# Attention edges of a graph network: products with y in cyclic order, some kept in PSUM, narrower maps, weights split over the rows of the array

## What is computed

```python
def _cg_tp(s, v, y0, y1, w_ss, w_sv, w_vs, w_vv0, w_vv1):
    out_s = concat([w_ss * s * y0, w_vv0 * dot(v, y1) / SQRT3])
    out_v = concat([(w_sv * s) * y1, w_vs * v * y0, w_vv1 * cross(v, y1) / SQRT2])
    return (out_s, out_v)

msg_s = (s_n @ Ws_src)[src] + (s_n @ Ws_dst)[dst]
msg_v = (v_n @ Wv_src)[src] + (v_n @ Wv_dst)[dst]
w1 = rbf @ W_rbf
m1_s, m1_v = _cg_tp(msg_s, msg_v, y0, y1, *split(w1))
a = (m1_s @ W_alpha).reshape(e, H, AS_)
a = where(a > 0, a, 0.2 * a)
a = sum(a * alpha_dot, axis=-1)
val_s = m1_s @ Ws_val
val_v = (m1_v @ Wv_val) * sigmoid(val_s @ Wg)[..., None]
val_s = sigmoid(val_s)
m2_s, m2_v = _cg_tp(val_s, val_v, y0, y1, w2_ss, w2_sv, w2_vs, w2_vv0, w2_vv1)
h = concat([m2_s @ Ws_vlin, m2_v @ Wv_vlin])
agg = segment_sum(segment_softmax(a, dst) * h, dst)
out = node + concat([agg_s @ Wps, agg_v @ Wpv])
```

## Time and profile before

| | |
|---|---|
| median of 3 runs | 9351.54 us (9351.42 to 9352.2) |
| the profiled execution | 9350.73 us, its span 9349.0 us |
| busy share of the span | PE 88%, PEld 70%, DVE 86%, ACT 57%, POOL 62% |
| constants, input and tables | about 0 to 228 us |
| attention edges | about 228 to 5322 us |
| softmax | about 5322 to 5456 us |
| aggregate | about 5480 to 6345 us |
| output, second layer's tables | about 6345 to 6690 us |
| conv edges, then the end | about 6690 to 9130, to 9349 us |

### The profile page before, as it was taken

The page is one execution under the profiler, slowest core; times in us unless marked ns, Lnnn a source line. Parts: engine busy times, 40 slices in busy tenths (PEclk is TensorE's granted clock), DMA queues, the critical chain, the costliest instruction groups (busy, mean ns, idle before and its releaser), DMA issues. The chain is left out here.

```text
span 9349.0 us, 200867 instructions
## 1 busy us (share of the span) xinstructions
PE 8247.1 (88%) x48376; PEld 6585.1 (70%) x48376; DVE 8021.4 (86%) x21707; ACT 5330.8 (57%) x17719; POOL 5808.5 (62%) x5949
## 2 busy tenths in 40 slices
PE   5999999999999999999999947775688888888885
PEld 2788888888888888888888836663355555555555
DVE  3899999999999999999999865554599999999993
ACT  1566666666666666666666611111377777777771
POOL 0776666666666666666666347770277777777760
PEclk5999999999999999999999979995699999999995
DMA  1443333333333334343333336660233333333330
GB/s 64 107 106 104 103 104 103 104 103 104 102 104 102 104 102 104 102 105 102 105 102 104 85 101 177 177 179 13 52 91 89 89 89 89 89 89 89 88 80 17
DMA packets 932683, 916.70 MB, mean 98 GB/s; under 512 B 370528, under 2 KB 734688, under 8 KB 931744
## 3 DMA queue, kind: packets, MB, share of 16 engines
q1 hardware_dynamic: 690208, 498.68, 19.4%
q0 software_dynamic: 241920, 413.20, 18.1%
HBM read 762.86 MB, written 148.44 MB: 97 GB/s over the span
## 5 line engine op out<-in xcount | busy, mean ns | idle before, releaser
L464 POOL DMA_INDIRECT ae_gsrc<-tab_src,ae_idx x1616 | 1641.9, 1016 | 1281.1 <-DVE ae_msg L583 567.0
L1096 POOL DMA_INDIRECT ce_node<-tab_conv,ce_idx x1808 | 1708.4, 945 | 1059.9 <-issue 645.5
L467 POOL DMA_INDIRECT ae_gdst<-tab_dst,ae_idx x1616 | 1819.6, 1126 | 538.6 <-issue 538.6
L1186 PE MATMUL psum<-ce_prod,ce_plain 128*128 128x384 f32 x3616 | 1540.5, 508 | 337.7 <-DVE ce_prod L1159 275.7
L1171 ACT ACTIVATE ce_prod<-ce_raw,ce_y 128x64 f32<-128x64 f32 x5424 | 1464.4, 333 | 0.0
L596 PE MATMUL psum<-pack_sb,ae_rbfy 80*128 80x352 f32 x3232 | 1161.5, 461 | 21.1 <-DVE ae_minus L494 13.2
L616 PE MATMUL psum<-pack_sb,ae_first_t 128*128 128x288 f32 x3232 | 1118.4, 428 | 41.3 <-ACT ae_first_t L689 8.8
L1169 ACT ACTIVATE ce_prod<-ce_raw,ce_y 128x160 f32<-128x160 f32 x1808 | 752.8, 416 | 528.3 <-DVE ce_raw L1118 528.3
L1188 PEld LDWEIGHTS psum<-ce_prod,ce_plain 128*128 128x128 f32 x3616 | 688.0, 190 | 479.9 <-issue 2.1
L681 ACT ACTIVATE ae_mapped<-psum 128x192 f32<-128x192 f32 x808 | 267.6, 331 | 1287.0 <-PE psum L618 1287.0
L903 POOL TENSOR_TENSOR ag_exval<-ag_val,alpha 128x256 f32<-128x256 f32 (+1 forms) x904 | 638.3, 726 | 403.6 <-DMA ag_val<-h_dram 399.1
(11 more groups left out here) (169 smaller groups left out, 21056.3 us busy)
## 6 DMA issues: line engine op xcount, KB each, us to landing
ag_val<-h_dram SPq DMA_DIRECT2D x452, 320.0 KB, 3.2
h_dram<-ae_values SPq DMA_DIRECT2D x404, 320.0 KB
ae_rbf<-in_rbf SPq DMA_DIRECT2D x404, 160.0 KB
ce_query<-in_query SPq DMA_DIRECT2D x452, 128.0 KB
ae_y<-in_y SPq DMA_DIRECT2D x404, 128.0 KB
ce_node<-tab_conv,ce_idx POOLq DMA_INDIRECT x1808
ae_gsrc<-tab_src,ae_idx POOLq DMA_INDIRECT x1616
ae_gdst<-tab_dst,ae_idx POOLq DMA_INDIRECT x1616
```

What stands on the lines that cost most here:

```text
L464: pool.indirect_dma_start(gsrc[t.slot4][:, k, :], None, g["tab_src"], bass.IndirectOffsetOnAxis(ap=idx[t.pair][:, t.odd, k:k + 1], axis=0))\
L467: pool.indirect_dma_start(gdst[t.slot4][:, k, :], None, g["tab_dst"], bass.IndirectOffsetOnAxis(ap=idx[t.pair][:, t.odd, 4 + k:5 + k], axi ...
L1096: pool.indirect_dma_start(node[t.slot8][:, k, :], None, g["tab_conv"], bass.IndirectOffsetOnAxis(ap=idx[t.slot8][:, k:k + 1], axis=0))\
L1186: pe.matmul(b_a[t.slot], plain[t.slot4][:, k, :], prod[t.slot][:, k, 96:480], start=(k == 0), stop=False, skip_group_check=True)
```

## The change

The message's vector part is multiplied with y1 at three offsets of a row of y that repeats itself cyclically (1, 2, 3, 1, 2). That gives the terms of the dot product (`diag`) and both halves of the cross product (`plus`, `minus`) before the weights are applied, so `wy` has 224 columns in place of 352. `minus`, the rows of y (`ya`, `yb`, `yc`) and `adot` lie in PSUM bank 7, which DVE alone uses; `b_h` shrinks to bank 6 and is filled in two halves. The radial values lie in 32 rows (16 of them times y0, 16 plain) for two k at a time, and the four weight matmuls of a tile use alternate groups of 32 rows, all at one place in PE's program. The values' s times y1 parts move behind the maps, as y enters there by linearity; the leaky part of the logits is a relu on ACT plus a linear part that is folded into the map (`m1_0`, four more columns), and the maps are 196, 96 and 96 columns. In the second round all three blocks have 128 rows, every matmul has 96 columns, and the matmuls of a tile come a body later and stand between the transposes. `gated` lies in the space of the nodes, so the nodes are loaded again in the aggregate; the square of y1 for every edge (`yy`) is computed once in `constants` from a load of all y. The order inside the vector part of h is x, head, channel, for which POOL reads a widened copy of alpha (`wide`) that ACT makes.

The diff, cut:

```diff
@@ constants
+                sp.dma_start(yraw[:, :, :], io["yall"]).then_inc(loaded, 16)
...
+                link(dve.tensor_tensor(ysq[:, :, :], yy4[:, :, 1:4], yy4[:, :, 1:4], ALU.mult))
+                link(dve.tensor_reduce(g["yy"][:, :], ysq[:, :, :], AX, ALU.add))
@@ attention_edges, DVE
-                def products(t, half):
...
+                        for d, out in enumerate((diag[:, :, 0:3, :], plus[:, :, :, :], minus)):
+                            ins = dve.tensor_tensor(out, v, cyclic(ya, d), ALU.mult)
+                        ins.then_inc(outer_done, 1)
...
+                        dve.tensor_tensor(gated[t.slot4][:, :, 0:8:2, :], comps(mapped[t.slot][:, :, 68:196]),
+                                          gated[t.slot4][:, :, 12:13, :].to_broadcast([P, 4, 4, CV]), ALU.mult)\
+                            .then_inc(gate_done, 1)
...
+                        dve.wait_ge(pe_weights, t.n + 1)
...
+                        dve.tensor_tensor(out[:, :, CS:96], b_w[:, :, P:160], dot[:, :, :], ALU.mult).then_inc(first_done, 1)
@@ attention_edges, PE
-                        pe.matmul(b_m[:, i, 0:288], first_t[1][:, e], w("m1_1"), start=True, stop=False)
-                        pe.matmul(b_m[:, i, 0:192], first_t[0][:, e], w("m1_0"), start=False, stop=False)
-                        ins = pe.matmul(b_m[:, i, 192:288], first_t[2][0:V3, e], w("m1_2"), start=False, stop=True)
+                        pe.matmul(b_m[:, i, 0:196], first_t[0][:, e], w("m1_0"), start=True, stop=False)
+                        pe.matmul(b_m[:, i, 196:292], first_t[1][:, e], w("m1_1"), start=False, stop=False)
+                        ins = pe.matmul(b_m[:, i, 164:260], first_t[2][0:V3, e], w("m1_2"), start=False, stop=True)
                     ins.then_inc(pe_mapped, 1)
+
+                def values_of(t, half):
+
+                    wait(pe, values_kept, 2 * t.n + half)
+                    for i in range(2):
+                        e = slice(P * (2 * half + i), P * (2 * half + i) + P)
+                        pe.matmul(b_h[:, i, 0:96], second_t[0][:, e], w("m2_0"), start=True, stop=False, skip_group_check=True)
+                        pe.matmul(b_h[:, i, 96:192], second_t[1][:, e], w("m2_1"), start=False, stop=False, skip_group_check=True)
+                        ins = pe.matmul(b_h[:, i, 32:P], second_t[2][:, e], w("m2_2"), start=False, stop=True, skip_group_check=True)
+                    ins.then_inc(pe_values, 1)
...
-                        pe.wait_ge(weighted, 2 * t.n + 1)
-                        weights(t, 1, 0)
+                    t = m + -4
+                    if t.inside(SUPER):
+                        pe.wait_ge(kept2, 3 * t.n + 3)
+                        values_of(t, 0)
...
+                        wait(pe, first_done, t.n)
+                        for k in (0, 2, 1, 3):
+                            q, e = 64 * t.slot + 32 * (k // 2), P * (k % 2)
+                            ins = pe.matmul(b_w[:, k, :], rbfy_both[q:q + 32, e:e + P], w("wy")[q:q + 32, :], start=True, stop=True)
+                        ins.then_inc(pe_weights, 1)
@@ attention_edges, ACT
+                    t = m + -4
+                    if t.inside(SUPER):
+                        wait(act, values_done, t.n - 1)
+                        wait(act, stored[t.slot4], 16 * t.quarter)
+                        keep_values(t, 0)
...
+                        for k in range(4):
+                            ins = act.activation(second[t.slot][:, k, 32:224].rearrange("p (b c) -> p b c", c=CV), gated[t.slot4][:, k, 0:12:2, :],
+                                                 ACT.Identity,
+                                                 scale=y[t.slot8][:, k, 0:1])
+                        ins.then_inc(scaled, 1)
+                    t = m + -3
+                    if t.inside(SUPER):
+                        keep2(t, 2)
@@ attention_aggregate
+                sp.dma_start(g["nodes"][:, :, :], io["x"]).then_inc(nodes_in, 16)
...
+                    pool.wait_ge(ex_done, t.n + 1)
+                    pool.tensor_tensor(exval[t.slot4][:, :, CS:C].rearrange("p k (x c) -> p k x c", c=AV),
+                                       val[t.slot8][:, :, CS:C].rearrange("p k (x c) -> p k x c", c=AV),
+                                       wide[t.slot4][:, :, :].unsqueeze(3).to_broadcast([P, 4, 3 * H, AV]), ALU.mult)\
+                        .then_inc(weighted, 1)
```

450 lines of the change are left out of this document (228 added, 222 removed), and 6 rows, old and new, of the table PACK.

## The result

The changed kernel takes 9369.29 us (median of 19 executions, 9366.18 to 9376.17), the kernel before 9351.43 (19 executions beside it). The ratio is 1.0019, 95% interval 1.0012 to 1.0026: 0.19% slower, just inside the 0.2% that the prediction called no difference. Forecast were 9024 us and a range up to 9230.

A forecast was written before the change was run, and what follows sets the result against it. PE bound the kernel before; after, a PE-ACT circle of 11.59 us plus 0.15 made 11.74 us a tile against 12.61, 351 us less over 404 tiles; with 23 added elsewhere, 9024 us, range 8790 to 9230.

The forecast's parts named there:

- The circle: Edge stage: PE and ACT wait for each other in a round of 11.59 us a tile, which sets the rate.
- the 0.15: Edge tile: estimate for three engine loops lying close together and for returns of the loop, added to 11.59 us.
- The sum: Edge tile: 9.13 us of PE work and some 2.5 of PE waiting for ACT, 11.59 together.
- Rival C: Edge stage: gaps in PE's work let the clock fall to 0.50; 20.8 us a tile, 12,680 us, chance 0.04.
- DVE: 10.6 to 11.1 forecast: Edge stage: DVE's work a tile in us, 8260 elements in 28 instructions plus up to 0.5 more.
- The room for DVE in the circle: Edge tile: DVE lets the weights' product be through by 4.9 us, and PE asks for it at 9.0.
- POOL: right: Edge stage: eight gathers a tile, 10.0 to 11.0 us in all, below what sets the rate.
- The 20 us: Constants: loading all y, its squares and sums, and small steps add 20 us on the path.
- its 9 us for the load of y: Constants: loading all y, 3.3 MB, takes 9 us, taken from 5.7 MB landing after 15.8 us.
- inside the bound: Aggregate: the second multiplication's new form costs between -0.1 and +0.5 us a step; 0 to +45 us, taken as 2.
- 0.90 for faster: Whole kernel: chance that the change makes it faster; same had 0.04, slower 0.06.
- Rival D: Edge stage: an unseen ACT or DVE wait makes the round 12.1 to 12.5 us; 9220 us, chance 0.12.

The follow-up runs named there:

- The exchanged order: Changed kernel with ACT's third copy of `turn2` put ahead of its four multiplications by y0: 9131.96 us, ratio 0.9765.
- the halved multiplications: Changed kernel with two of ACT's four multiplications by y0 left out (k = 2 and 3): 9136.24 us, ratio 0.9772.

## Why the prediction was wrong

**What bounded the kernel: right.** PE was the bound before, and its busy time fell by 672 us. The stretch after the second round is what the prediction described: the narrow maps, `turn2`, the weights in 1.03.

**The circle: the mechanism right, the sizes 0.5 us short.** The waits that it named are there: 1.20 at the second `turn` (forecast 1.5) and 0.20 to 0.28 at the second half of the second round (forecast 0.4). The one of 0.49 at the first `turn` it did not name. The exchanged order and the halved multiplications show that this circle sets the rate: with half of them the tile fell to 11.49. The legs can be read off ACT, which starts each:

```profile
3084.31 0.28 ACT L704 ACTIVATE ae_mapped<-psum 128x128 f32<-128x128 f32 x1 [1.85 <-PE psum L638]
...
3084.97 0.62 ACT L715 ACTIVATE ae_second_t<-psum 128x512 f32<-128x512 f32 x1
3085.44 1.50 ACT L763 ACTIVATE ae_second<-nodes,ae_y 128x192 f32<-128x192 f32 x4
3086.82 0.61 ACT L715 ACTIVATE ae_second_t<-psum 128x512 f32<-128x512 f32 x1
...
3089.49 0.38 ACT L721 ACTIVATE ae_values<-psum 128x256 f32<-128x256 f32 x1 [0.72 <-PE psum L648]
...
3096.40 0.28 ACT L704 ACTIVATE ae_mapped<-psum 128x128 f32<-128x128 f32 x1 [1.85 <-PE psum L638]
```

| leg | forecast | measured |
|---|---|---|
| ACT takes the maps out (3084.31 to 3084.97) | 0.73 | 0.66 |
| copy, four multiplications, copy, to PE (to 3087.49) | 2.54 | 2.52 |
| second turn, half of the second round (to 3089.49) | 1.82 | 2.00 |
| ACT copies it out (to 3090.10) | 0.65 | 0.61 |
| second half (to 3091.51) | 1.23 | 1.41 |
| maps, turn2, weights, maps (to 3096.40) | 4.62 | 4.89 |
| round | 11.59 | 12.09 |

ACT's legs are right to 0.07. PE's are 0.63 short, in four places:

- The second round, 0.26. A k of three matmuls of 96 columns was taken as 1.5 times the 0.41 of the earlier trace rows, 0.62. The four of a tile take 0.64, 0.67, 0.74 and 0.67 to the next start. A likely reason is that in the earlier trace rows the two matmuls of 96 follow one of 192, which covers part of the first one's start; the 0.74 stands right behind a wait.
- The weights, 0.18. Ahead of them `turn2` takes 0.54 where the same four transposes take 0.44 elsewhere (3093.07 to 3093.61, 3084.11 to 3084.55), and behind them the first pair of the maps takes 0.44 (3082.47 to 3082.91) where the second takes 0.36.
- From the last matmul of a block to ACT, 0.05 twice (0.20 for 0.15), and the second `turn` behind its wait, 0.05.
- The maps' own pace, 0.04 (0.78 a k for 0.77).

```profile
3082.47 0.60 PE L636 MATMUL psum<-pack_sb,ae_first_t 128*128 128x196 f32 x2
3082.91 0.36 PE L637 MATMUL psum<-pack_sb,ae_first_t 128*128 128x96 f32 x2
...
3084.11 0.60 PE L628 MATMUL psum<-pack_sb,ae_second 128*128 128x128 f32 x4
3084.55 0.60 PE L628 MATMUL psum<-pack_sb,nodes 128*128 128x128 f32 x4
...
3093.07 0.60 PE L628 MATMUL psum<-pack_sb,ae_second 128*128 128x128 f32 x4
3093.61 1.03 PE L685 MATMUL psum<-pack_sb,ae_rbfy 32*128 32x224 f32 x8
```

So going into and out of the weights costs 0.18 us, 73 us over the stage, which the prediction took as nothing because the earlier trace rows showed none.

The Trainium skill, page TensorEngine Tiling (Array Packing), section Tiling Modes, which the prediction weighed there, says that a change of tiling mode drains the TensorE. The trace agrees in kind, with 0.18 us where the prediction worked out 0.25 by that rule.

Against the 0.15 that the prediction added for returns of the loop (which cost nothing here), the circle is 0.36 us a tile over 11.74, 145 us. That alone would have left a time of about 9170, within the range.

**The clock: the step that failed.** The sum takes all of PE's work at the clock of 1.00, with some 2.5 us of waiting in each tile, 1.5 of it in one piece, and puts what the waits do to the clock at nothing. Rival C had the mechanism, gaps in PE's work, with a chance of 0.04 and a price of thousands of us, because it thought of one level for the whole stage. Its argument against itself counted matmul instructions in a us, and compared averages of stages: 6.8 here, more than in the aggregate, which holds its clock. What came was between: falls in four tiles of ten, 0.53 us a tile, 214 us. The average of a stage did not show it; the falls stand behind one pair of waits in the tile, and the larger of the two, 1.5 us, was in the prediction's own sum.

The Trainium skill has a like case, on a page that the prediction did not weigh: TensorE: Matmul & The Clock Gate, section A second HAM failure mode: psum-queue depth-cycling, tells of a bf16 kernel that cycles through PSUM banks, whose short idle times between groups of matmuls make the clock go to and fro between its two levels. The trace agrees in an fp32 kernel, with 0.49 and 1.20 us of waiting for the banks of the turns, and a clock of 0.50 behind them.

145 and 214 us are 359, and the profiled execution is 353 over the forecast (9376.17 us against 9023). The aggregate is 21 less than forecast; the other 15 us, the other way, lie mostly in the edges and the softmax and were not traced to a cause.

**DVE: 10.6 to 11.1 forecast, 11.45 or a little more measured** (where it sets the rate). The pace of products was right. The sum over four products was taken at 1.04 ns an element, 0.60 us, and takes 0.95 to the next start:

```profile
3053.07 1.05 DVE L583 TENSOR_REDUCE ae_second<-ae_diag 128x128 f32<-128x512 f32 x1
3054.02 0.55 DVE L590 TENSOR_TENSOR ae_path<-ae_values,psum 128x384 f32<-128x384 f32 x1
```

Two additions in its place brought what their rows promised, 158 us in a kernel where DVE was the bound. The room for DVE in the circle was right: no wait of PE for DVE in the changed kernel.

**POOL: right.** The gathers take 963 and 965 ns, near the lower value of the earlier trace rows (945). The Trainium skill's rule on the shared port (page SBUF — State Buffer, section Who interferes with whom) is that a DVE instruction with two SBUF inputs contends with a GpSimd instruction that reads SBUF, and one with at most one SBUF input, outside the 2-port modes, does not. The trace agrees in direction, since most products now read one input from PSUM. No run here changed that alone, so the cause is not shown.

**Constants and aggregate.** The 20 us were 19.1. Of the 5.7 MB behind its 9 us for the load of y, shows only the nodes' 3.9. The aggregate's form without a row costs 849 ns where the old one took 830, inside the bound; that the stage got 19 us shorter was not expected and has no explanation here.

**The chances.** 0.90 for faster rested on the sum and on the range of the sum. The step that failed was no term of it. Rival D's price does not follow from its own period, either: 12.1 to 12.5 us is 9170 to 9330, with a middle of 9250, not 9220.

## What to carry to other kernels

When a change turns an engine's full stretch into work with waits, price TensorE's clock with it: list the waits of one tile in order, and treat long ones that lie close together as a risk, whatever the stage's average (here falls stood behind 0.49 and 1.20 us, none behind 0.49 and 0.51, and in the kernel before none behind a single 1.23); if they can't be removed, work in the wait is the cheapest test and may be the remedy. Then ask of each engine off the path what its stops (at a loop's return, here 4 us) will cost on the day it becomes the bound. And take the pace of a short instruction from a run of short ones, not from one that follows a long one.

## What the runs showed of the hardware that I had not expected

- Useless work can pay: 1.3 us of it a tile, in a wait of 1.2, made the kernel 2.1% faster (9369 to 9172) by holding the clock at 1.00.
- A single wait of 1.23 us a tile did not lower the clock in the kernel before (no fall in 245 tiles); two, of 0.2 to 1.0 and 1.45 to 1.83, did in 20 of 35. In the changed kernel 0.49 and 1.20 did in 125 of 309, and 0.49 and 0.51, with half of ACT's multiplications, did not.
- DVE stops for 3.6 to 4.7 us when its loop returns, 4.0 on the mean, whether the loop is 8 or 32 tiles long (155.8 us in 39 times, 39.5 in 10); in the kernel before (`DVE ae_first L486 <- issue: 78.8, 40, 2.2`) 2.0 each. Why it doubled with the change stays open.
- Eight passes of 224 columns take 0.96 us in two groups of 32 rows, 1.71 in one group and 1.52 with all 128 rows; the order of the four multiplications made no difference.
